# Attention and mixture of experts on one core: a finer first norm, one prefix scan, another order of the units in a step

## What is computed

```python
xn = layernorm(x)                       # x: 32 x 256 x 128, no gamma and beta here
# attention: 16 heads of 8 channels, causal, on xn
qkv = xn @ w_qkv
attn = softmax(mask(q @ k.T / sqrt(8)))
y = xn + (attn @ v) @ w_proj + b_proj
attention = layernorm(y) * ln_gamma + ln_beta
# mixture of experts: 8 experts, the best 2 for each token, on the same xn
probs = softmax(xn @ Wr.T)
ffn = sum over the top 2: probs[e] * (gelu(xn @ W1[e] + b1[e]) @ W2[e] + b2[e])
out = x + attention + ffn
```

## Time and profile before

| | us |
|---|---|
| median of 3 runs | 849.73 |
| the 3 runs | 847.44 to 850.27 |
| the profiled execution's own time | 851.77 |
| its span, first to last instruction | 850.0 |
| PE busy | 699.9 (82%) |
| DVE busy | 692.9 (82%) |
| ACT busy | 525.4 (62%) |
| POOL busy | 536.0 (63%) |
| mean granted PE clock | 0.958 of full speed |

### The profile page before, as it was taken

The page is one execution under the profiler, slowest core; times in us unless marked ns, Lnnn a source line. Parts: engine busy times, 40 slices in busy tenths (PEclk is TensorE's granted clock), DMA queues, the critical chain, the costliest instruction groups (busy, mean ns, idle before and its releaser), DMA issues.

```text
span 850.0 us, 24989 instructions
## 1 busy us (share of the span) xinstructions
PE 699.9 (82%) x7877; PEld 518.1 (61%) x7878; DVE 692.9 (82%) x1617; ACT 525.4 (62%) x1039; POOL 536.0 (63%) x575
## 2 busy tenths in 40 slices
PE   1366579999999999999888888868999999999800
PEld 1243346666666666666655555537888889888800
DVE  5778878898999998989889999557788888888744
ACT  4541346565656565656556565537989999999800
POOL 8750456767676776767777777334767676667710
PEclk9999899999999999999999999978999999999955
DMA  8294122232323232232233432202222222222189
GB/s 220 80 400 122 64 84 94 81 111 79 114 77 111 80 111 94 94 98 90 84 127 107 139 125 78 64 7 62 84 85 80 85 88 84 82 82 82 56 266 335
DMA packets 113313, 93.66 MB, mean 110 GB/s; under 512 B 16618, under 2 KB 97650, under 8 KB 113268
## 3 DMA queue, kind: packets, MB, share of 16 engines
q1 hardware_dynamic: 95508, 70.26, 27.0%
q0 software_dynamic: 8704, 18.17, 5.9%
q10 hardware_dynamic: 9056, 4.66, 1.9%
HBM read 43.85 MB, written 48.93 MB: 109 GB/s over the span
## 4 chain that ended last, share of the span: by engine, by line
PE 56%; DVE 13%; issue 7%; POOL 7%; DMA 6%; ACT 5%; SPq 5%; DVEq 0%; ACTq 0%; POOLq 0%
PE wide L1259 10%; PE bank_head L1148 7%; PE wide L1113 5%; PE bank_head L1250 5%; PE bank_maxB L1250 5%; PE bank_maxA L1127 4%; PE bank_maxB L1127 3%; DMA xn_rows<-parts_dram 3%; DMA k_cat<-qk_rows 3%; DVE shift L911 3%; POOL probs L581 3%; PE bank_misc L1173 3%; SPq L478 2%; PE bank_maxB L1131 2%; PE bank_maxA L1131 2%
## 5 line engine op out<-in xcount | busy, mean ns | idle before, releaser
L581 POOL TENSOR_SCALAR_AFFINE_SELECT probs<-probs 128x512 f32<-128x512 f32 (+1 forms) x192 | 158.3, 833 | 103.6 <-ACT probs L653 102.8
L653 ACT ACTIVATE probs<-wide 128x1024 f32<-128x1024 f32 x192 | 188.8, 1018 | 47.3 <-PE wide L1117 24.5
L619 POOL DMA_INDIRECT parts_dram<-o_T,dest x144 | 161.0, 1118 | 74.7 <-issue 48.6
L572 POOL DMA_INDIRECT x_slots<-xn_rows,slot_i x128 | 127.3, 995 | 62.8 <-DVE slot_i L868 31.4
L911 DVE TENSOR_REDUCE shift<-bank_maxA 128x2 f32<-128x512 f32 (+1 forms) x192 | 132.1, 688 | 20.1 <-PE bank_maxA L1131 12.9
L911 DVE TENSOR_REDUCE shift<-bank_maxB 128x2 f32<-128x512 f32 (+1 forms) x192 | 131.5, 685 | 4.9 <-PE bank_maxB L1131 0.8
L687 ACT ACTIVATE probs<-wide,b_all 128x256 f32<-128x256 f32 x288 | 121.4, 478 | 16.8 <-PE wide L1259 10.0
L1148 PE MATMUL bank_head<-probs,v_aug 128*32 128x256 f32 (+1 forms) x2048 | 98.9, 334 | 19.1 <-POOL probs L581 18.9
L1259 PE MATMUL wide<-xgT_raw,xnT 128*128 128x256 f16 x864 | 109.2, 277 | 3.7 <-DVE xgT_raw L1020 3.6
L1003 DVE TENSOR_TENSOR probs<-probs 128x512 f16<-128x512 f32 x144 | 99.7, 692 | 5.5 <-ACT probs L693 1.1
L1127 PE MATMUL bank_maxA<-k_cat,q_diag 128*128 128x128 f16 (+1 forms) x512 | 76.2, 252 | 28.5 <-DVE shift L911 19.5
(11 more groups left out here) (174 smaller groups left out, 1252.4 us busy)
## 6 DMA issues: line engine op xcount, KB each, us to landing
qk_rows<-split SPq DMA_DIRECT2D x32, 512.0 KB, 3.2
x_slots<-fill SPq DMA_DIRECT2D x16, 598.5 KB, 7.6
fill<-x_slots SPq DMA_DIRECT2D x72, 133.0 KB
q_diag<-qk_rows SPq DMA_DIRECT2D x256, 32.0 KB
k_cat<-qk_rows SPq DMA_DIRECT2D x64, 128.0 KB
xn_rows<-parts_dram SPq DMA_DIRECT2D x8, 1024.0 KB, 11.8
x_all<-in_x SPq DMA_DIRECT2D x8, 512.0 KB, 7.6
pieces_f<-in_w SPq DMA_DIRECT2D x8, 512.0 KB, 4.8
```

The costliest lines, as they stand in the source:

```text
L572: pool.indirect_dma_start(out=x_slots, out_offset=bass.IndirectOffsetOnAxis(ap=slot_i[:, t, c:c + 1], axis=0), in_=xn_rows[:, t, :], in_of ...
L581: pool.affine_select(out=part, in_=part, compare_op=ALU.is_ge, fill=0.0, base=0, pattern=[[0, n], [1, P]], channel_multiplier=-1).then_inc ...
L619: pool.indirect_dma_start(out=parts_dram, out_offset=bass.IndirectOffsetOnAxis(ap=dest[:, of, t:t + 1].bitcast(U32), axis=0), in_=y[:, of ...
L653: act.activation(probs[:, u, :], ps[:, :], ACT.Exp, scale=SCALE).then_inc(empty, 1)
```

## The change

1. **The first norm.** `MOMENTS` has six groups (8, 8, 8, 16, 16 and 8 tiles). ACT normalises 13 groups and DVE 3. The router's weights are loaded first, and PE waits for them alone, ACT for the qkv weights alone. POOL clears `q_diag` in other pieces between the powers. DVE reaches its part of step 0 after the statistics of all tiles, where it came before those of the last 8 tiles.
2. **`ln_beta`.** POOL adds four of the eight parts behind `picks` (during step 1), two at the end of step 2 and two at the end of step 3.
3. **Routing.** The counts come out expert by expert, so one scan of 512 elements takes the place of 8 of 64 elements. `goes_on` (0 at the first tile of each expert) restarts it, and the start of an expert is added to its first count. Five instructions that make the router's weights leave `places` for `weights`, which runs at the end of step 2, and become four. Sends begin in step 3 (`SEND = FINISH`), where they began in step 2.
4. **The order in a step.** `s5` stands ahead of `o0`. `proj` has moved to the next step (stage LAST), behind `m1`, with `add_and_measure`. On POOL the power stands behind `s0`, where it came at the end of the step. `last` of a row comes in the same step as its projection.
5. **From step 24.** In even steps the three tiles are sent at `m0`, `m0` and `s2` (before: `m0`, `s1`, `s3`). ACT takes the high part of a piece of expert weights behind `v`, no longer at the end of the step, and DVE the low part at the start of the next step.

SP's instructions and their order stay as they are, apart from two counts that it waits for.

```diff
-        SEND = SOFT
+        SEND = FINISH
         USES = [
-            ("maxA", "m0", MAXIMA), ("maxB", "m1", MAXIMA), ("misc", "qk", PROJECT),
+            ("maxA", "m0", MAXIMA), ("maxB", "m1", MAXIMA), ("head", "proj", LAST),
+            ("misc", "qk", PROJECT),
...
-            ("wide0", "s4", SOFT), ("maxB", "m11", MAXIMA), ("head", "o0", SOFT),
-            ("misc", "shift", MAXIMA), ("wide1", "s5", SOFT), ("head", "proj", FINISH),
+            ("wide0", "s4", SOFT), ("maxB", "m11", MAXIMA), ("wide1", "s5", SOFT),
+            ("head", "o0", SOFT), ("misc", "shift", MAXIMA),
         ]
...
-                places = ("m0", "s1", "s3") if (s - TAIL) % 2 == 0 else SEND_AFTER
+                places = ("m0", "m0", "s2") if (s - TAIL) % 2 == 0 else SEND_AFTER
...
-        ACT_GROUPS = 12
+        ACT_GROUPS = 13
-        MOMENTS = [(0, 8), (8, 16), (16, 32), (32, 48), (48, 64)]
+        MOMENTS = [(0, 8), (8, 16), (16, 24), (24, 40), (40, 56), (56, 64)]
...
# POOL
+            wait_normed(pool, ACT_GROUPS - 1)
+            wait_normed(pool, GROUPS - 1)
+            pool.wait_ge(weights_loaded, 64)
+            pool.wait_ge(route, ROUTE_PICKED + 1)
+            for c in range(BETA_PARTS // 2):
+                add_beta(c)
...
+                    if what == SUM_AFTER and has(s, LAST):
+                        powers(s)
                     if what == SUM_AFTER and has(s, FINISH):
                         sums(s)
-                if has(s, FINISH):
-                    b = s - FINISH
-                    pool.wait_ge(mv2_ready, b * 3 + 3)
-                    pool.tensor_tensor(rstd2[:, :], mv2[:, :, 1], half[:, 0:QT], ALU.pow).then_inc(rstd2_ready, 1)
+                if s in (2, 3):
+                    for c in range(2 * s, 2 * s + 2):
+                        add_beta(c)
...
# DVE, places
-                for e in range(E):
-                    V.tensor_tensor_scan(place[:, :, e], ones[:, :], total.rearrange("p (t e) -> p t e", e=E)[:, :, e],
-                                         padded[:, e:e + 1], ALU.mult, ALU.add).then_inc(route, 1)
+                then(V.tensor_tensor(first_tile_total, first_tile_total, padded[:, :], ALU.add))
+                then(V.tensor_tensor_scan(place_by_expert[:, :, :].rearrange("p e t -> p (e t)"), goes_on[:, :, :].rearrange("p e t -> p (e t)"), total, 0.0,
+                                          ALU.mult, ALU.add))
...
# DVE, the end of a step
+                if isinstance(s, int) and s == SOFT:
+                    weights()
                 if isinstance(s, int) and s == FINISH:
                     pack_experts()
```

More of the change, by code:

```diff
@@ L582, in mask, with powers @@
                                    pattern=[[0, n], [1, P]], channel_multiplier=-1).then_inc(probs_ready, 1)
+            def powers(s):
+                b = s - LAST
+                pool.wait_ge(mv2_ready, b * 3 + 3)
+                pool.tensor_tensor(rstd2[:, :], mv2[:, :, 1], half[:, 0:QT], ALU.pow).then_inc(rstd2_ready, 1)
             def sums(s):
                 b = s - FINISH
-                if has(s - 1, FINISH):
-                    made(pool, s - 1, "proj")
+                if has(s, LAST):
+                    made(pool, s, "proj")
                 pool.tensor_tensor(xpb[:, :, :], xn_all[:, bass.ds(b * QT, QT), :],
@@ L653, in exp, with high_piece @@
                 act.activation(probs[:, u, :], ps[:, :], ACT.Exp, scale=SCALE).then_inc(empty, 1)
+            def high_piece(i):
+                act.wait_ge(piece_loaded[i % 2], 16 * (i // 2 + 1))
+                act.activation(part_of(i, 0), piece[i % 2], ACT.Copy).then_inc(piece_high, 1)
             def step(s, par):
@@ L667, in step @@
                                        ps[:, 0:QT * D].rearrange("p (t h d) -> p t h d", t=QT, h=H), ACT.Copy).then_inc(empty, 1)
+                        for i in pieces(s):
+                            high_piece(i)
                     elif what in ("o0", "o1"):
@@ L678, in step @@
                         exp(s, int(what[1:]))
-                for i in pieces(s):
-                    act.wait_ge(piece_loaded[i % 2], 16 * (i // 2 + 1))
-                    act.activation(part_of(i, 0), piece[i % 2], ACT.Copy).then_inc(piece_high, 1)
             def hidden(s, par, e, half_):
@@ L870, in places, with weights @@
                 assert route_count == ROUTE_DONE, route_count
+            def weights():
+                nonlocal route_count
+                dve.wait_ge(exp_router, 2)
+                then(V.tensor_reduce(red[:, :], prob[:, :, :], axis=AX.X, op=ALU.add))
+                V.tensor_scalar(xn_rows[:, :, D + 4], best[:, 0, :], -1.0, float(E), ALU.mult, ALU.add).then_inc(route, 1)
+                route_count += 1
+                then(V.reciprocal(xn_rows[:, :, D], red[:, :]))
+                then(V.scalar_tensor_tensor(out=xn_rows[:, :, D + 2], in0=top[:, 1, :], scalar=-1.0, in1=xn_rows[:, :, D],
+                                            op0=ALU.add, op1=ALU.mult))
+                assert route_count == ROUTE_WEIGHTS, route_count
             packing_count = 0
@@ L953, in last @@
                 dve.wait_ge(rstd2_ready, b * 1 + 1)
+                if isinstance(s, int) and s == LAST:
+                    dve.wait_ge(offset_ready, BETA_PARTS)
                 for t in range(QT):
```

109 lines of the change are left out of this document (63 added, 46 removed).

## The result

| | before | changed |
|---|---|---|
| median of 5 runs (us) | 848.76 | 857.88 |
| the runs | 845.94 to 850.27 | 855.45 to 860.30 |
| the profiled execution's own time | 851.77 | 860.30 |
| its span | 850.0 | 858.4 |

The ratio is 1.0108, with a 95% interval of 1.0075 to 1.0141: the change costs 9 us. Each of the two lies 2 to 3 us above its kernel's median.

What follows compares the result with a forecast made beforehand. The prediction took a chain from `o0` through `shift`, ACT, SP's transfers and their landing to `m6` to bound the steady steps. Terms -9.5 + 3.3 + 6.7 + 0.8 - 0.5 = +0.8 us gave 850.5 us, range 843 to 858.

Steps and rivals of the forecast that it cites:

- The likeliest case: Whole kernel: the start's gain pays for the longer steps; 850.5 us, spanning 847 to 854, chance 0.39.
- The rival in which the transfer chain pays in full: Steady steps: landing not shortened, since SP's and POOL's traffic still overlap; 0.55 us per step, 856.5 us, chance 0.33.
- start up to `o0`(3): Up to step 2: SP leaves its fills earlier, so the second store and step 2 come earlier; -9.5 us.
- packing: DVE's packing ahead of step 4: loses a wait for PE, but POOL's masks and moved additions hold it; +3.3 us.
- 19 steady steps: Steps 4 to 23: `s5` delays `o0` by 0.5 to 0.6 us, a shorter landing returns part; +0.35 each, +6.7 us.
- from step 24: Steps from 24 on: transfer waits and drawn-out SP issues cost, shorter waits for POOL's masks gain; +0.8 us.
- handover and behind: Handover to the first slot tile: `proj` and DVE's low part leave its front, a read comes behind; -0.5 us.
- The idea that DVE sets the pace: Steady steps: DVE, not the transfer, sets the pace, so its shorter wait gains 0.25 us each; 838 us, chance 0.08.
- five steps with the transfer's price: From step 24: five steps wait for the transfer and pay 0.35 to 0.5 us each; +2 us.
- -2 for the masks' waits: From step 24, even steps: waits for POOL's masks, like that of `o1`, go; -2 us in all.
- +0.8 for the sends: From step 24: four sends in a row at `m0` lie beside SP's issues and can draw them out; +0.8 us.

Runs made afterwards that it cites:

- fills_early: The changed kernel with the 16 fills issued right behind the input's loads, ahead of step 0: 855.29 us, ratio 1.0046 to the kernel before.
- beta_ahead: The changed kernel with all eight additions of `ln_beta` on POOL ahead of step 2: 851.91 us, ratio 1.0035 to the kernel before.
- sends_late: The changed kernel with a memset of about 1.2 us on POOL ahead of the sends at `m0` in steps 5 to 23: 865.15 us.
- before_s5_first: The kernel before with `s5` ahead of `o0` as its only edit: 868.61 us, ratio 1.0238.
- order_back: The changed kernel with the whole order of units as before (`s5`, `proj` and POOL's power back), the new start kept: 841.89 us, ratio 0.9905.
- joined: The changed kernel with `s5` behind `shift` again, all `ln_beta` additions ahead of step 2, DVE's low part of weights behind `add_and_measure`: 843.25 us.
- s5_back: The changed kernel with only `s5` moved back behind `shift`: 847.00 us, ratio 0.9972 to the kernel before.

## Why the prediction was right or wrong

The measured 857.88 us lies in the range (843 to 858), at its very end. The likeliest case, 850.5 us, did not happen: I forecast no change (0.37) a little ahead of slower (0.35), and it was slower. The rival in which the transfer chain pays in full gave 856.5 us and came nearest, though not for its own reason: it holds from +0.45 us a step on, and the steps pay 0.42. That the time lies inside the range is partly luck. Term by term, in the profiled executions:

| term | predicted | bounds | measured |
|---|---|---|---|
| start up to `o0`(3) | -9.5 | -12 to -7 | -8.6 |
| packing | +3.3 | -2.2 to +5.5 | +5.5 |
| 19 steady steps | +6.7 | 0 to +11 | +8.0 |
| from step 24 | +0.8 | -3 to +6 | +5.3 |
| handover and behind | -0.5 | -2 to +1 | -1.8 |
| sum | +0.8 | | +8.4 |

**The start: right, with two misses that nearly cancel.** The fills came 1.9 us later (2.6 predicted) and took the same time, and the second store went at 70.54 (71.4). From the store to `m0` it then took 10.0 us (80.53), where the sum had 8.0: SP issues the transfers that read the store only at 76.49, 5.95 us behind it, and not after 3.2 to 3.7. (The sum's 82.4 for `m2` is 82.2 by its own terms; it was 83.28.) The 14.7 us of earlier preparation didn't reach the end. `fills_early` shows the mechanism: take the fills away and the store goes at 59.

**The packing: right in kind, its size was wrong.** I let one instruction through per POOL instruction and laid five of ten with two SBUF operands behind them. What was held was one instruction with a single SBUF operand, through two masks and both additions, and nothing got through between them; the measured +5.5 is the upper bound. The Trainium skill (SBUF — State Buffer, section "SBUF: two separate sides") says that DVE, in a 2-port mode or with two SBUF inputs, and GpSimd take the shared port pair for a whole instruction and that the other fully blocks. By that rule the +3.3 us stood in the sum rather than the -2.2. The traces agree that POOL's work holds DVE: 6.28 us beside the additions, 1.68 us beside the masks alone. They show more than one instruction's hold, though: an addition takes 2.3 us, and DVE was held through two masks and both additions. With the additions away, `o0`(3) to `o0`(4) takes 19.3 us in `beta_ahead`, as in the kernel before (19.4), so the additions are the whole +5.5.

**The steady steps: right.** `s5` costs 0.63 us (0.5 to 0.6 predicted), SP's intervals stayed at 2.50, 4.39 and 4.80 us, and the landing gave back 0.23 of it (0 to 0.35). Two steps together take 28.8 us, as forecast. `sends_late` shows that the sends' earlier end is what shortens the landing. The idea that DVE sets the pace is out: DVE releases the bank of `m6` at least 0.6 us ahead of the landing, and `before_s5_first` pays the whole price of `s5`.

**From step 24: this step failed.** The sum had +0.8 us, and +5.3 were measured, more than half of the whole miss of 7.6 us. Two of its terms were mis-sized in opposite ways. I took five steps with the transfer's price, +2; in `beta_ahead`, whose code from step 24 on is that of the changed kernel, this part takes 141.1 us, and with `s5` back 137.0 in `order_back` and `joined`, all at a mean clock of 1.00: +4.1, near to 9 steps by the 0.42 us of the steady steps. I took -2 for the masks' waits and +0.8 for the sends; the edits other than the order bring -3.6 (140.6 to 137.0). Together these make +0.5, so the forecast of +0.8 would have held by cancelling.

What the sum had nothing for is the clock. The profiled execution of the changed kernel takes 4.8 us more here than `beta_ahead`, and all but 0.1 us of it stands in the three steps that hold the stretches of 3.4 us at the lower level: +1.6, +0.7 and +2.3 us. Half of 3.4 us is 1.7, so the clock alone can't be the whole of the third, which also has a longer wait for `k_cat` ahead of it (3.28 us, against 2.5 at most in `beta_ahead`). `fills_early`, again with the same code here, has two such stretches and takes 145.0 us. So this cost comes in some executions and not in others. The waits of `o1` for DVE's read of `proj`, which I had named and laid nothing on, are not its price by themselves: they are 13.4 us in `beta_ahead`, 13.2 in the changed kernel and 14.0 in `s5_back`, which takes 137.5 us with one slow stretch. That they bring the clock down is only argued. And `before_s5_first` paid only 1.1 us in its tail; why is open.

**The handover** gave 1.8 us, within its bounds; no run tells what in it.

The chances were the weak place: all three terms with a plus sign came out above what I took, and all for costs laid on a chain. A gain ahead of the steps is worth what the next wait leaves of it; a cost in the chain is paid in every step.

## What to carry to other kernels

Before moving an instruction ahead of another on one engine, find the instruction whose result starts the next round of the longest chain: 0.6 us of work ahead of it cost 11 us over the whole kernel here, and the wait that it could cure, that of `o1` for the mask of `s5`, was 0.2 us a step (0.25 and 0.19 in steps 11 and 12 of the kernel before). Put bulk work of POOL where DVE waits for something else, and bulk transfers where the queues are idle, here right behind the input's loads. And judge a change of many parts part by part: all but its new order gained 7 us, and the order cost 16.

## What the runs showed of the hardware

- A DVE instruction on 72 columns took 0.20 us beside one of POOL's sends, 1.68 us beside masks, and 6.28 us beside a run of masks and additions, and not the time of one of them (2.3 us); in `order_back` it got through after the first addition, in 2.15 us. What decides that is open.
- From the issue of a 128 KB transfer to the matmul that waited for it, it took 2.3 to 2.4 us when POOL's indirect sends had ended a microsecond ahead of the issue, 2.6 to 2.8 us when they ended about as it was issued, and 2.5 to 2.65 us when they ended a microsecond behind its start.
- 16 fills of 598 KB each took 19.33 us of SP's issue right behind the input's loads and 18.68 us later: the queue takes the same time, and the place decides who stands behind it. The first store, issued behind them at 34.56, let its readers go only at 48.57, and yet step 1's `shift` came just 0.6 us later on PE (67.08 against 66.47).
- Four small transfers cost ACT's queue 2.42 us, as much as SP's, and everything of ACT behind them is held for it.
- PE's granted clock was at its lower level (0.50, 1.2 GHz) for 3.4 us from 490.1 and from 507.2 us, after waits of PE of 2.10 and 2.42 us (busy for 2.06 of the 4 us from 487, for 1.58 of the 4 us from 503); it stood at 1.00 through this part in the kernel before, and in `beta_ahead` too, whose code is the same here.
